# A fused decoder layer on one core: gate chain in PSUM, VectorE reordered, context blocks loaded early, layer norms applied by ScalarE

## What is computed

```
x = x + attn(layernorm(x))                # one head: scores, piecewise factor by bands of sigmoid, softmax, projection
x = x + xattn(layernorm(x), ctx, ctx)     # 8 heads of 32; gates, decay matrix, group norm
x = x + ffn(layernorm(x))                 # 256 -> 1024 -> 256, exact gelu, low-rank adapters made from tokens 1 to 16

xattn: itilde, ftilde = [q, k, v] @ Wi, Wf + bias        # per head and position
       csum = cumsum(log_sigmoid(ftilde))
       D[i, j] = exp(csum_i - csum_j + itilde_j - max_j(...)) for j <= i
       C = (q k^T) * D / tau;  H = C v / (max(|sum C|, exp(-max)) + 1e-6)
       out = (H - mean) / sqrt(var + 1e-5) per head, times gn_w, plus gn_b
```

## Time and profile before

| | |
|---|---|
| median of 3 runs | 1925.06 us |
| profiled execution | 1924.64 us, span 1922.9 us |
| TensorE busy | 1809.3 us, 94% |
| VectorE busy | 1571.9 us, 82% |
| ScalarE busy | 1081.1 us, 56% |
| GpSimd busy | 335.0 us, 17% |
| DMA | 75.57 MB, mean 39 GB/s |

### The profile page before, as it was taken

How to read it: one execution, slowest core, us unless ns; L and a number is a source line. 1 busy time by engine, 2 the same in 40 slices (tenths; PEclk the granted TensorE clock), 3 DMA queues, 4 the chain that set the end, 5 groups by cost and what they waited for, 6 DMA issues and landing times.

```text
span 1922.9 us, 44190 instructions
## 1 busy us (share of the span) xinstructions
PE 1809.3 (94%) x14040; PEld 1362.2 (71%) x14040; DVE 1571.9 (82%) x4524; ACT 1081.1 (56%) x2440; POOL 335.0 (17%) x269
## 2 busy tenths in 40 slices
PE   5589999999999999999999999999999999999988
PEld 4457777777777777777777777777777777777766
DVE  6687888898888888888889888888888888888752
ACT  1355566555566655556655556665556665555552
POOL 2121121122022112112112102211211211210210
PEclk9789999999999999999999999999999999999999
DMA  4101111111111111111111111111111111111100
GB/s 119 31 28 26 35 45 47 39 42 25 44 36 47 47 36 46 25 35 45 47 38 44 24 42 39 47 47 36 46 25 35 45 47 37 45 24 39 32 15 25
DMA packets 205743, 75.57 MB, mean 39 GB/s; under 512 B 150273, under 2 KB 205186, under 8 KB 205714
## 3 DMA queue, kind: packets, MB, share of 16 engines
q1 hardware_dynamic: 205714, 75.21, 15.1%
HBM read 53.93 MB, written 16.78 MB: 37 GB/s over the span
## 4 chain that ended last, share of the span: by engine, by line
PE 77%; DVE 10%; issue 7%; ACT 5%; DMA 0%; SPq 0%; DVEq 0%; ACTq 0%
PE UA L1376 17%; PE UB L1376 5%; PE TB L1453 3%; PE GT L1386 3%; DVE bands L965 3%; PE TA L1343 3%; PE TA L1453 3%; PE UB L1318 3%; PE TA L1283 3%; PE TA L1184 3%; PE TB L1184 3%; PE UA L1318 3%; ACT QKs L694 3%; PE PV L1318 2%; PE UB L1420 2%
## 5 line engine op out<-in xcount | busy, mean ns | idle before, releaser
L1376 PE MATMUL UA<-W2f,hs_all 128*128 128x256 f32 x1536 | 350.8, 381 | 3.8 <-DVE ot L1022 3.1
L1376 PEld LDWEIGHTS UA<-W2f,hs_all 128*128 128x128 f32 x1536 | 286.5, 190 | 67.0 <-ACT hs_all L704 14.1
L1039 DVE TENSOR_TENSOR C<-qT,QKs 128x512 f32<-128x512 f32 x256 | 166.2, 690 | 113.7 <-ACT qT L713 104.4
L598 POOL TENSOR_TENSOR Ng<-HT,gnw_b 128x256 f32<-128x256 f32 x128 | 105.4, 824 | 823.2 <-ACT HT L726 823.2
L579 POOL TENSOR_TENSOR xg<-x,gnb_b 128x1024 f32<-128x1024 f32 x32 | 83.9, 2621 | 682.6 <-ACT ot L668 645.6
L1376 PE MATMUL UB<-W2f,hs_all 128*128 128x256 f32 x512 | 115.8, 379 | 0.0
L612 ACT ACTIVATE lv<-ve 128x4 f32<-128x4 f32 x95 | 19.1, 202 | 164.2 <-DVE ve L831 164.2
L694 ACT ACTIVATE QKs<-TA 128x512 f32<-128x512 f32 x64 | 38.4, 600 | 125.3 <-PE DD L1343 125.3
L1376 PEld LDWEIGHTS UB<-W2f,hs_all 128*128 128x128 f32 x512 | 95.0, 190 | 11.7
L1343 PEld LDWEIGHTS TA<-xn2T,ctxT 32*128 32x128 f32 x512 | 63.3, 190 | 43.6 <-issue 41.1
L1343 PE MATMUL TA<-xn2T,ctxT 32*128 32x128 f32 x512 | 74.9, 286 | 19.3 <-DVE acs L969 17.1
(11 more groups left out here) (328 smaller groups left out, 5146.2 us busy)
## 6 DMA issues: line engine op xcount, KB each, us to landing
xin<-x SPq DMA_DIRECT2D x32, 512.0 KB, 3.4
ctxn<-ctx SPq DMA_DIRECT2D x32, 512.0 KB, 3.5
bands<-ctx SPq DMA_DIRECT2D x256, 64.0 KB, 1.9
out<-ot SPq DMA_DIRECT2D x32, 512.0 KB, 3.0
Ev<-xn SPq DMA_DIRECT2D x512, 1.0 KB
hs_all<-L_ffn_W SPq DMA_DIRECT2D x4, 512.0 KB, 8.4
E<-xn SPq DMA_DIRECT2D x128, 16.0 KB
T<-tok SPq DMA_DIRECT2D x128, 8.0 KB, 1.7
```

The source lines that it names most:

```text
L598: pool.tensor_tensor(Ng[:, b, :].rearrange("p (k n) -> p k n", k=2), HT[:, b % 2, :, 0:P], gnw_b[:, :].rearrange("p (k n) -> p k n", k=2), ...
L1039: dve.tensor_tensor(C[:, b % 2, :, half], dx[hf].rearrange("p (h i) -> p h i", h=HEADS), QKs[:, b, :, half], ALU.mult)\
L1376: ins = pe.matmul(OB[b][:, 0:D], hs_all[:, k, b * S:(b + 1) * S], W2f[:, k, :], start=(i == 0), stop=(i == KH - 1))
```

## The change

It does seven things. The two tiles gabs and lsig become columns 128 to 383 of bank GT. VectorE's first two band instructions move behind the decay rows; the copy acs gets the running maximum as a third part, by a scan that reads one operand from the bank, and the tile am goes. The eight block loads get a tile of their own and are issued near the start of the step, and the transpose into ctxT moves ahead of the products of block 0. The context group is loaded straight into vc, at the end of a step, and changed in place, with one more GpSimd instruction that sets the last dimension of each head to one. ScalarE copies the QK banks in another order, and the first two decay products each wait for their own bank. VectorE's scale of layer norm 0 moves behind the products of block 1. And the mean and scale of all layer norms in the steps are applied by ScalarE as Identity activations, with a fifth small instruction in ln_scale that makes the shift.

The diff, cut to its core (VectorE's own ln_apply goes as well, and the setup keeps its four instructions for the first group):

```diff
+        one = sb("one", [P, 1])
...
-        ctx_blocks = bands[:, :, :].rearrange("p k (n c) -> p k n c", c=32)
...
-        ctxn = sb("ctxn", [P, G, D])
+        blocks = sb("blocks", [P, 2, N])
+        ctx_blocks = blocks[:, :, :].rearrange("p k (n c) -> p k n c", c=32)
...
-        gabs = sb("gabs", [P, P])
-        lsig = sb("lsig", [P, P])
...
-        acs = sb("acs", [32, 2 * P])
-        am = sb("am", [32, 2, P])
+        acs = sb("acs", [32, 3, P])
...
+        shift = [sb(f"shift{i}", [P, G]) for i in range(3)]
...
+        gabs, lsig = GT[:, P:2 * P], GT[:, 2 * P:3 * P]
...
                 if FFN.on(it):
                     t_rows(it)
+                if SELF.on(it):
+                    sp.wait_ge(ctxT_ok.h, ctxT_ok.at(it, 0))
+                    for h in range(HEADS):
+                        sp.dma_start(ctx_blocks[32 * (h % 4):32 * (h % 4) + 32, h // 4, :, :],
+                                     c_blocks[it][:, :, 32 * h:32 * h + 32]).then_inc(blocks_loaded.h, 16)
                 if COMING.on(it):
                     sp.wait_ge(xb_ok.h, xb_ok.at(it, 1))
                     sp.dma_start(xin[:, :, :], x_g[it + 1]).then_inc(x_loaded.h, 16)
-                if SELF.on(it):
-                    sp.wait_ge(vc_ok.h, vc_ok.at(it, 1))
-                    sp.dma_start(ctxn[:, :, :], c_g[it]).then_inc(ctx_loaded.h, 16)
...
-                if SELF.on(it):
-                    sp.wait_ge(y_ok.h, y_ok.at(it, 1))
-                    for h in range(HEADS):
-                        sp.dma_start(ctx_blocks[32 * (h % 4):32 * (h % 4) + 32, h // 4, :, :],
-                                     c_blocks[it][:, :, 32 * h:32 * h + 32]).then_inc(blocks_loaded.h, 16)
                 if CROSS.on(it):
                     e_rows(it)
+                if SELF.on(it):
+                    sp.wait_ge(pv_mm.h, pv_mm.at(it, G))
+                    sp.dma_start(vc[:, :, :], c_g[it]).then_inc(ctx_loaded.h, 16)
                 if FFN.on(it):
                     sp.wait_ge(ot_ok.h, ot_ok.at(it, G))
                     sp.dma_start(o_g[it - 2], ot[:, :, :]).then_inc(stored.h, 16)
...
                 if CROSS.on(it):
                     pool.wait_ge(ctx_loaded.h, ctx_loaded.at(it, 0))
-                    pool.wait_ge(pv_mm.h, pv_mm.at(it, 0))
-                    heads = ctxn[:, :, :].rearrange("p b (h d) -> p (b h) d", h=HEADS)
-                    pool.tensor_tensor(vc[:, :, :].rearrange("p b (h d) -> p (b h) d", h=HEADS)[:, :, 0:HD - 1],
-                                       heads[:, :, 0:HD - 1],
+                    heads = vc[:, :, :].rearrange("p b (h d) -> p (b h) d", h=HEADS)
+                    pool.tensor_tensor(heads[:, :, 0:HD - 1], heads[:, :, 0:HD - 1],
                                        heads[:, :, HD - 1:HD].broadcast_to([P, G * HEADS, HD - 1]),
-                                       ALU.subtract).then_inc(vc_ok.h, 1)
+                                       ALU.subtract).then_inc(diff_ok.h, 1)
+                    pool.wait_ge(diff_ok.h, diff_ok.at(it, 1))
+                    last = heads[:, :, HD - 1:HD]
+                    ones = one[:, 0:1].unsqueeze(1).broadcast_to([P, G * HEADS, 1])
+                    pool.tensor_tensor(last, ones, ones, ALU.mult).then_inc(vc_ok.h, 1)
...
+            def ln_apply(i, it, X, Xn, free):
+
+                act.wait_ge(rs_ok[i].h, rs_ok[i].at(it, 1))
+                for f, k in free:
+                    act.wait_ge(f.h, f.at(it, k))
+                for b in range(G):
+                    src, dst = X[:, b, :], Xn[:, b, :]
+                    if i == 2:
+                        src = src.rearrange("p (u c) -> p c u", c=CB)
+                        dst = dst.rearrange("p (c u) -> p c u", c=CB)
+                    ins = act.activation(dst, src, ACT.Identity, bias=shift[i][:, b:b + 1], scale=rs[i][:, b:b + 1])
+                ins.then_inc(xn_ok[i].h, 1)
...
                 if CROSS.on(it):
                     act.wait_ge(gate_ok.h, gate_ok.at(it, 1))
-                    a.link(act, act.activation(gabs[:, :], gate[:, :], ACT.Abs))
-                    a.link(act, act.activation(lsig[:, :], gabs[:, :], ACT.Exp, scale=-1.0, bias=cut[:, 0:1]))
-                    act.activation(gabs[:, :], lsig[:, :], ACT.Ln, bias=1.0).then_inc(lnsig_ok.h, 1)
+                    a.link(act, act.activation(gabs, gate[:, :], ACT.Abs))
+                    a.link(act, act.activation(lsig, gabs, ACT.Exp, scale=-1.0, bias=cut[:, 0:1]))
+                    act.activation(gabs, lsig, ACT.Ln, bias=1.0).then_inc(lnsig_ok.h, 1)
...
-                    for r in range(4):
+                    for r in (3, 1, 0, 2):
...
                     hs(3)
+                if coming:
+                    ln_apply(0, it, xin, xn1, [(score_mm, 1), (px_mm, 2)])
+                if cross:
                     ht(3)
...
                     ln_root(2, it)
+                    ln_apply(2, it, x3, xn3, [(xn3T_mm, 2), (e_loaded, 0), (ev_loaded, R * G * 16)])
                 if coming:
                     evac_qT(it, 0)
                     evac_qT(it, 1)
                 if own:
                     ln_root(1, it)
+                    ln_apply(1, it, x2, xn2, [(xn2T_mm, 2), (x2_ok, G)])
...
                 link(dve.tensor_tensor(rs[i][:, :], nt[i][:, :], rs0[i][:, :], ALU.mult))
...
+                dve.scalar_tensor_tensor(shift[i][:, :], mean[i][:, :], -1.0, rs[i][:, :], ALU.mult, ALU.mult)\
+                   .then_inc(rs_ok[i].h, 1)
...
                     dve.wait_ge(lnsig_ok.h, lnsig_ok.at(it, 1))
-                    link(dve.scalar_tensor_tensor(lsig[:, :], gate[:, :], cap[:, 0:1], gabs[:, :], ALU.min, ALU.subtract))
-                    dve.tensor_tensor_scan(csum[:, :], carry[:, :], lsig[:, :], 0.0, ALU.mult, ALU.add)\
+                    link(dve.scalar_tensor_tensor(lsig, gate[:, :], cap[:, 0:1], gabs, ALU.min, ALU.subtract))
+                    dve.tensor_tensor_scan(csum[:, :], carry[:, :], lsig, 0.0, ALU.mult, ALU.add)\
                        .then_inc(csum_ok.h, 1)
 
-                if own:
-                    dve.wait_ge(sc_ok.h, sc_ok.at(it, 1))
-                    band_lo = v.mark(dve.tensor_scalar(band_a[:, :], sc[:, :], BANDS[0], 0.3, ALU.is_ge, ALU.mult))
-                    band_hi = v.mark(dve.tensor_scalar(band_b[:, :], sc[:, :], BANDS[3], None, ALU.is_gt))
                 if cross:
                     dve.wait_ge(sel_mm.h, sel_mm.at(it, 1))
-                    dve.tensor_copy(acs[:, :], DD[0:32, 0:2 * P]).then_inc(acs_ok.h, 1)
+                    link(dve.tensor_copy(acs[:, 0:2, :].rearrange("p a n -> p (a n)"), DD[0:32, 0:2 * P]))
+                    dve.tensor_tensor_scan(acs[:, 2, :], acs[:, 1, :], DD[0:32, P:2 * P], -3e38,
+                                           ALU.max, ALU.max).then_inc(acs_ok.h, 1)
                     dve.wait_ge(acs_ok.h, acs_ok.at(it, 1))
-                    run_max = v.mark(dve.tensor_tensor_scan(am[:, 1, :], acs[:, 0:P], acs[:, 0:P], -3e38,
-                                                            ALU.max, ALU.max))
-                    dve.tensor_copy(am[:, 0, :], acs[:, 0:P])
-                    dve.wait_ge(v.h, v.upto(run_max))
                     dve.wait_ge(em_mm.h, em_mm.at(it, 0))
-                    arg = v.mark(dve.tensor_tensor(em[0:32, :], am[:, 1, :], acs[:, P:2 * P], ALU.add))
-                    neg = v.mark(dve.tensor_scalar(am[:, 1, :], am[:, 1, :], -1.0, None, ALU.mult))
+                    arg = v.mark(dve.tensor_tensor(em[0:32, :], acs[:, 2, :], acs[:, 0, :], ALU.add))
+                    neg = v.mark(dve.tensor_scalar(acs[:, 2, :], acs[:, 2, :], -1.0, None, ALU.mult))
...
                 if own:
+                    dve.wait_ge(sc_ok.h, sc_ok.at(it, 1))
+                    band_lo = v.mark(dve.tensor_scalar(band_a[:, :], sc[:, :], BANDS[0], 0.3, ALU.is_ge, ALU.mult))
+                    band_hi = v.mark(dve.tensor_scalar(band_b[:, :], sc[:, :], BANDS[3], None, ALU.is_gt))
                     dve.wait_ge(v.h, v.upto(band_lo))
...
-                def apply0():
-                    dve.wait_ge(score_mm.h, score_mm.at(it, 1))
-                    dve.wait_ge(px_mm.h, px_mm.at(it, 2))
-                    ln_apply(0, xin, xn1)
-
                 if coming:
                     dve.wait_ge(x_loaded.h, x_loaded.at(it, 16))
                     ln_stats(0, xin, link)
+                if own:
+                    dve.wait_ge(blocks_loaded.h, blocks_loaded.at(it, HEADS * 16))
+                    dve.wait_ge(qk_mm.h, qk_mm.at(it, 2))
+                    dve.transpose(ctxT[:, :, :].rearrange("p k n -> p (k n)"),
+                                  blocks[:, :, :].rearrange("p k n -> p (k n)")).then_inc(ctxT_ok.h, 1)
                 if cross:
                     weigh_qk(0, 0)
                     weigh_qk(0, 1)
                 if ffn:
                     gT_copy()
+                if cross:
+                    weigh_qk(1, 0)
+                    weigh_qk(1, 1)
                 if coming:
```

(32 more changed lines are left out.)

11 lines of the change are left out of this document (2 added, 9 removed).

## The result

The changed kernel takes 1958.88 us (median of 4 runs, 1958.11 to 1961.11) against 1924.64 us of the kernel before on the same chip (4 runs): a ratio of 1.018, 95% interval 1.0164 to 1.0199. The forecast was 1889.6 us with a range of 1878 to 1906. The sign is wrong, and none of the rivals describes what happened.

A forecast was written before the change was run, and what follows sets the result against it. TensorE's queue was taken to bound the 56.89 us step, with 1.54 us idle. Gains of 0.07 + 0.65 + 0.37 + 0.13 = 1.22 us over 29 steps, 35.4 us, gave 1889.6 us, range 1878 to 1906.

The forecast's parts named there:

- Layer norms on ScalarE: 12 added ScalarE instructions: four between hs(3) and ht(3), eight at the step's end; claimed to fit and cost nothing.
- ht(3) still waits for TensorE: Sign expected in the profile after: ScalarE's four layer norm 0 activations, about 0.4 us each, end before ht(3) can start.
- given back at the step's end: Rival: ScalarE finishes xn2 or xn3 late, its first copy of the next step slips 1.2 us; about 1924, chance 0.04.
- Ends of the run: First and last steps: 1.6 us added once in step 0, some 1 us saved before the gram product; set to 0.
- Gate chain and order of VectorE: Gate stretch: PSUM gate chain gains 0.07 us a step at up(4), reordered VectorE 0.65 at qk(0).
- the rival in which it is: Rival "It doesn't do what it says": the scan still held by GpSimd; 1891 us, inside the forecast, no separate chance.
- Decays: New QK bank order: decays start about 0.3 us sooner, but down(0) still waits for bank UA; gain taken as 0.

The follow-up runs named there:

- first experiment: The changed kernel with all three layer norms applied by VectorE again, all other edits kept: 1896.82 us, ratio 0.985 to the kernel before.
- last nudge: All layer norms on VectorE in the changed kernel, plus two 4-element VectorE instructions between Er and Ef, each waited for: 2058.18 us, ratio 1.070.

## Why the prediction was wrong

- *Layer norms on ScalarE, the step that failed.* "So they fit, with 0.4 us to spare, and cost nothing" was worked out for the four of layer norm 0. In the loop they cost nothing, but by luck: the four take 2.06 us where 1.97 were idle, and ht(3) follows without a gap at 1041.81, just as its product is there (on TensorE, 1041.16 to 1041.77). The sign "ht(3) still waits for TensorE" did not come.

```profile
1039.74 2.06 ACT L630 ACTIVATE xn<-xin,shift,rs 128x256 f32<-128x256 f32 x4
1041.81 0.39 ACT L744 ACTIVATE HT<-UB 128x264 f32<-128x264 f32 x1
```

  For one instruction was priced at the 0.39 us of a 264 element copy, with 0.69 as the upper bound. Grouped by tile, the changed kernel has:

```profile
L630 ACT ACTIVATE xn<-xg,shift,rs 128x256 f32<-128x256 f32 x128 | 98.2, 842 | 37.4 <-DVE shift L862 37.4
L630 ACT ACTIVATE xn<-x,shift,rs 128x256 f32<-128x256 f32 x128 | 66.4, 589 | 35.1 <-DVE shift L862 35.1
L630 ACT ACTIVATE xn<-xin,shift,rs 128x256 f32<-128x256 f32 x124 | 63.9, 588 | 0.0
```

  0.59 us, and 0.84 us with the stride of layer norm 2, outside the bound. The larger fault is the sentence behind it, that the other eight "run at the end of the step", where only the qT copies are queued behind them. Behind layer norm 1 the next instruction of ScalarE's queue is the xn3T copy of the following step. The list of what is queued behind the waiting instruction stopped at the loop's edge. The 1.99 us of idle time were no cover: they lie before the copy, layer norm 1 waits for its root and scale and begins inside them, only 0.71 us ahead of the score product, and then takes 2.08 us. The runs showed what that costs, 1.89 us a step: 0.93 for the late gram product and 0.96 for Ef behind xg.
- *The rival "given back at the step's end"* names the right place (the xn3T copy slips) but stops at 1924 us, for it knows only the first of the two costs; 1929.38 us with xg held back is that case. The second, Ef against xg, is in no rival, though the profile before showed two such meetings in the gate stretch (the scan and the first band) and a third that was missed by 0.09 us.
- *Ends of the run*, set to nothing: 13.2 us (9.7 before step 2, 3.5 behind the last score product). The layer norms on ScalarE account for 9.8 (6.0 and 3.8, first experiment), of them 5.0 in step 0, the wait of 2.85 us with a lower clock behind it. Most of the rest differs from profile to profile whatever the edit: the first score product starts between 27.6 and 31.2 us (here 1.3 us later than before), and with all layer norms on VectorE step 0 takes 43.3 us in some profiles and 45.1 in others.
- *Gate chain and order of VectorE*: right in the main. Of the forecast 1.22 us a step, 0.96 came. By the distances between TensorE's starts, all layer norms on VectorE: up(4) 0.04 us later (forecast 0.07 earlier), qk(0) 0.63 closer to it (0.65), 0.06 lost again up to down(0), pv(1) 0.37 closer to adapt(0) (0.37), pv(3) 0.07 (0.13). The scan was not held in PSUM, so the rival in which it is has fallen. But the terms are not a sum of parts: tried alone they gave 0.65 (bands), 0.29 (PSUM) and 0.01 (scale). Beside the reorder the gate chain in PSUM shows no gain: qk(0) starts 13.09 us behind the score product with the bands moved alone, and 13.15 with all edits but the layer norms.
- *Decays* 0, as forecast, and down(0) keeps its distance from qk(0).

## What to carry to other kernels

An instruction moved to an idle engine has to be placed in that engine's queue across the loop's edge: the next one behind it may belong to the next step and be the head of its longest chain. The mean busy share of the engine (56% here) says nothing on that. Where two engines exclude each other, look also at the pairs that just miss each other, and fix their order with a wait on the engine that has time; here that wait, on GpSimd, costs nothing that these runs can tell. And try edits in the combination in which they are meant: an edit worth nothing alone (the scale) can be half of one that pays.

## What the runs showed of the hardware

- A VectorE instruction with two SBUF reads and a GpSimd instruction wait for each other, whoever comes second: Ef 2.39 us instead of 0.48, or xg 2.65 to 2.96 us instead of 2.42. The bands, which read one tile (128x512, TENSOR_SCALAR), were held as well, 2.00 us instead of 0.42, and even an instruction on 4 elements took 2.36 us instead of 0.23. The scan with one operand in PSUM was not held (0.42 us). By the Trainium skill, page "SBUF — State Buffer", section "Who interferes with whom", the two exclude each other for the whole length of an instruction; the rows agree, and add that instructions that follow without a gap kept the other engine out (xg 2.96 us), while a gap of 0.14 us (between Er and Ef in the changed kernel) or 0.04 us (between the two tiny instructions) was enough to lose the turn.
- A hold repeats itself: where GpSimd has another instruction queued, it starts about when the held VectorE instruction ends, and the next one of VectorE can be held again (2.33 and 1.91 us for the bands with the gate chain in PSUM, 2.36 and 2.67 us in the last nudge).
- ScalarE's Identity from SBUF to SBUF with a scale and a bias per partition takes 0.59 us for 256 elements (0.52 from start to start), 0.84 with both sides strided; VectorE applied the same layer norms in 0.41 us, 0.51 with both sides strided.
- After TensorE had stood still for 0.52, 1.49 and 1.26 us within 5 us, the granted clock was 0.50 (its 1.2 GHz level) for one window of 4 us and 0.66 in the next. The waits of 0.89 and 1.16 us in the changed kernel, 10.6 us apart, left it at 1.00. Waits of 0.86 and 1.91 us, 10.7 us apart (the kernel before with the layer norms on ScalarE), left it at 1.00 in 17 steps and brought it to 0.80 to 0.89 and 0.68 to 0.77 in two windows of 4 us in 11 others, though the waits were the same.
